# Linear-recurrence block on one core: paired 64x64 tiles for two products, narrower powers, and work moved between engines

## What is computed

```
xx  = shift(x) - x
lo  = tanh((x + xx*maa_x) @ maa_w1)            # 4 groups of 32
xm[g] = x + xx * (lo[g] @ maa_w2[g] + maa[g])  # four mixed inputs: rg, wa, k, v
r, k, v = xm_rg @ Wr, xm_k @ Wk, xm_v @ Wv     # 512x512 each
g = tanh(xm_rg @ gate_w1) @ gate_w2 ;  w, a, ma, mk, kk: low-rank gates and a normalised key
step:  sa = S a ;  S = S * w + sa b^T + v k^T ;  y = S q      # S: 32x32 per head
y = group_norm(y) * ln_w + ln_b + (sum(r*k*faaaa)) * v
out = feed_forward(y * g @ Wo)                 # layer norm, int8 rows, 512x512, scale, bias, residual
```

## Time and profile before

| | |
|---|---|
| median of 3 runs | 3234.14 us (3229.86 to 3235.64) |
| profiled execution | 3244.0 us, span 3242.2 us |
| PE busy / PEld busy | 3029.1 us (93%) / 2675.6 us (83%), 84224 instructions each |
| DVE / ACT / POOL busy | 2626.5 (81%) / 1974.8 (61%) / 1270.6 us (39%) |
| chain that ended last | PE 92%, issue 3%, ACT 2%, DVE 2% |
| DMA queue of SP | 6.8% of the 16 engines; x tile 128 KB, 2.7 us to landing |
| ACT_TABLE_LOAD | 383 at L504 and 64 at L643, 1283 ns each |

### The profile page before, as it was taken

How to read it: one execution, slowest core, us unless ns; L and a number is a source line. 1 busy time by engine, 2 the same in 40 slices (tenths; PEclk the granted TensorE clock), 3 DMA queues, 4 the chain that set the end, 5 groups by cost and what they waited for, 6 DMA issues and landing times.

```text
span 3242.2 us, 182735 instructions
## 1 busy us (share of the span) xinstructions
PE 3029.1 (93%) x84224; PEld 2675.6 (83%) x84224; DVE 2626.5 (81%) x5443; ACT 1974.8 (61%) x3519; POOL 1270.6 (39%) x1161
## 2 busy tenths in 40 slices
PE   6999999999999999999999999999999999999996
PEld 5888888888888888888888888888888888888884
DVE  4788888888888888887888888887888878888875
ACT  3575675665665665755656656656567566566563
POOL 4334334334334344343344343443433434433332
PEclk9999999999999999999999999999999999999998
DMA  3000000000000000000000000000000000000000
GB/s 118 10 23 20 17 23 19 18 20 18 22 20 17 23 20 17 23 20 17 22 20 19 20 17 23 20 17 23 20 17 23 20 17 20 20 20 20 16 17 19
DMA packets 39380, 70.47 MB, mean 22 GB/s; under 512 B 9812, under 2 KB 10836, under 8 KB 38616
## 3 DMA queue, kind: packets, MB, share of 16 engines
q1 hardware_dynamic: 38616, 58.77, 6.8%
HBM read 41.97 MB, written 16.78 MB: 18 GB/s over the span
## 4 chain that ended last, share of the span: by engine, by line
PE 92%; issue 3%; ACT 2%; DVE 2%; POOL 0%; POOLq 0%; ACTq 0%; DVEq 0%
PE bank L1070 30%; PE bank_a L1209 12%; PE bank L1273 8%; PE bank_a L1187 4%; PE bank L1077 4%; PE bank_b L1187 4%; PE bank_b L1244 3%; PE bank_b L1237 3%; PE bank_a L1237 3%; PE bank_a L1244 3%; PE bank_a L1217 2%; PE bank_a L1225 2%; PE bank L1123 2%; PE bank_a L1263 2%; PE bank_b L1263 2%
## 5 line engine op out<-in xcount | busy, mean ns | idle before, releaser
L504 ACT ACT_TABLE_LOAD x383 | 491.4, 1283 | 19.1 <-DVE shift L761 12.2
L1070 PE MATMUL bank<-xm_rg,w_r 128*128 128x128 f32 x2048 | 285.4, 282 | 4.3 <-issue 3.5
L504 ACT ACTIVATE u<-bank_a,parity 128x256 f32<-128x256 f32 x128 | 53.7, 471 | 386.7 <-PE bank_a L1253 386.7
L1209 PE MATMUL bank_a<-pw,w_ffn_int 32*32 32x64 f32 x16384 | 264.6, 216 | 22.0 <-issue 17.2
L1273 PE MATMUL bank<-w_o,yc 128*128 128x512 f32 x512 | 268.9, 626 | 11.0 <-DVE yc L744 9.3
L1209 PEld LDWEIGHTS bank_a<-pw,w_ffn_int 32*32 32x32 f32 x16384 | 239.6, 106 | 41.7 <-issue 21.3
L1070 PEld LDWEIGHTS bank<-xm_rg,w_r 128*128 128x128 f32 x2048 | 248.9, 191 | 26.8 <-issue 15.9
L504 ACT ACTIVATE u<-bank_b,parity 128x256 f32<-128x256 f32 x128 | 53.8, 471 | 342.3 <-PE bank_b L1253 342.3
L1070 PEld LDWEIGHTS bank<-xm_k,w_k 128*128 128x128 f32 x2048 | 241.2, 194 | 12.5 <-issue 3.8
L1070 PE MATMUL bank<-xm_v,w_v 128*128 128x128 f32 x2048 | 250.2, 275 | 0.0
L1070 PE MATMUL bank<-xm_k,w_k 128*128 128x128 f32 x2048 | 241.7, 277 | 3.5 <-issue 3.5
(11 more groups left out here) (204 smaller groups left out, 8540.4 us busy)
## 6 DMA issues: line engine op xcount, KB each, us to landing
xin<-in_x SPq DMA_DIRECT2D x128, 128.0 KB, 2.7
xres<-in_x SPq DMA_DIRECT2D x128, 128.0 KB
out<-o_sb SPq DMA_DIRECT2D x128, 128.0 KB, 2.4
w_ffn_int<-in_weight_q SPq DMA_DIRECT2D x1, 2048.0 KB, 10.8
w_k<-in_Wk SPq DMA_DIRECT2D x1, 1024.0 KB
w_r<-in_Wr SPq DMA_DIRECT2D x1, 1024.0 KB
w_v<-in_Wv SPq DMA_DIRECT2D x1, 1024.0 KB
w_o<-in_Wo SPq DMA_DIRECT2D x1, 1024.0 KB, 14.2
```

Of the source, the lines that this page charges most:

```text
L504: return nc.scalar.activation(out_, in_, func, **kw)
L1070: ins = mm(bank[:, o * n:(o + 1) * n], weights[:, k, o * P:(o + 1) * P], x[:, k].rearrange("p b t -> p (b t)"), start=(k == 0), stop=(k == ...
L1209: ins = mm(bank_a[q, 64 * n:64 * n + 64], pt[q, g, :], source[q, g, 0:2].rearrange("p j t -> p (j t)"), start=True, stop=True)
```

## The change

On TensorE:

1. `scores` replaces `scores_b` and `scores_k`. For each group the two key products follow the two removal products, and they write the other half of the partitions of bank_b, so that the four products of a group stand in four different 64x64 tiles. `scores` now waits for both a_b2 and a_k2 at its start.
2. `first_state_second_values` interleaves, in the same way, the state products of chunk 0 (bank_b) with the value products of chunk 1 (bank_a). `first_values` and `second_state` stay alone.
3. The powers stream 32 columns (k = 0) and 48 columns (k = 1, 2) instead of 64; `pw` is [P, G, 3, HALF].
4. The order of the step is rearranged.

So that the operands lie where the off-diagonal tiles want them, Wv is loaded with its 64-column halves swapped (8 DMAs instead of 1), and two new pairs of DMAs per step on SP (`turn_keys`, `turn_values`) move kt and vT_raw to the other half of the partitions.

On the other engines: ScalarE expands each square into `spread` (two passes with a mask as scale) beside the copy pw, so that VectorE transposes from there; it adds maa for three of the four mix factors (12 passes of 128 columns), and VectorE keeps one multiply for each; it computes x2n with a bias that VectorE forms (`norm2_shift`). GpSimd forms the first sums (two adds), and tx. The orders of VectorE, ScalarE and GpSimd are rearranged too; in ScalarE's, `log_variance` and its function set come ahead of the `keys` copy, and `exp_tables` (a table load) stands between `solution(m, 0)` and `output_gate`.

```diff
-            def scores_b(m):
+            def scores(m):
                 pe.wait_ge(v_q, count(m, 1, 1))
                 pe.wait_ge(a_b2, count(m, 1, 1))
+                pe.wait_ge(a_k2, count(m, 1, 1))
                 pe.wait_ge(a_y, count(m, NC, 0))
-                scores(bank_a, bt2).then_inc(p_sb, 1)
...
+                for g in range(G):
+                    for h in range(QH // 2):
+                        q = two_heads(h)
+                        removal = mm(bank_a[q, 64 * g:64 * g + 64], both(bt2[q, g]), both(aq[q, g, 0:2]),
+                                     start=True, stop=True)
+                    for h in range(QH // 2):
+                        q = two_heads(h)
+                        key = mm(bank_b[other(q), 64 * g:64 * g + 64], both(kt2[q, g]), both(aq[q, g, 0:2]),
+                                 start=True, stop=True)
+                removal.then_inc(p_sb, 1)
+                key.then_inc(p_sk, 1)
...
+                    if k == 0:
+                        ins = mm(bank_a[q, 64 * n:64 * n + CHUNK], pt[q, g, :], first[q, g, 1, :], start=True, stop=True)
+                    else:
+                        ins = mm(bank_a[q, 64 * n:64 * n + 3 * HALF], pt[q, g, :],
+                                 pw[q, g].rearrange("p a t -> p (a t)"), start=True, stop=True)
...
+            def first_state_second_values(m):
+                pe.wait_ge(sold, count(m, NC, 1))
+                pe.wait_ge(v_t, count(m, 1, 1))
+                pe.wait_ge(p_values, count(m, 1, 1))
+                for j in range(GS):
+                    for h in range(QH // 2):
+                        ins = state_product(0, j, two_heads(h))
+                    for h in range(QH // 2):
+                        values_product(1, j, two_heads(h))
+                ins.then_inc(p_rhs, 1)
...
             def power(m, k):
                 act.wait_ge(p_pw, count(m, POWERS, k + 1))
-                run(pw[:, :, 0, :], pairs(bank_a)[:, :, 0, :], ACT.Copy).then_inc(a_pw, 1)
+                square = pairs(bank_a)[:, :, 0, 0:HALF]
+                act.wait_ge(v_ptT, count(m, POWERS + 1, k + 1))
+                run(spread[:, :, 0, :], square, ACT.Identity, scale=mask_half[:, 0:1])
+                run(spread[:, :, 1, :], square, ACT.Identity, scale=mask_half[:, HALF:HALF + 1]).then_inc(a_spread, 1)
+                run(pw[:, :, 0, :], square, ACT.Copy).then_inc(a_pw, 1)
...
+            def mix_factors(i, n):
+                act.wait_ge(p_xm, count(i, 1, 1))
+                act.wait_ge(mix_loaded, MIX_LOADED)
+                g = (1, 2, 3, 0)[n]
+                for k in range(KB):
+                    ins = run(xm[n][:, k], fb[MIX_BANK[n]][:, k * TOK:(k + 1) * TOK].rearrange("p (b t) -> p b t", b=B),
+                              ACT.Identity, bias=maa[:, g, k:k + 1])
+                ins.then_inc(a_xm, 1)
...
+            def turn_keys(i):
+                sp.wait_ge(v_k, count(i, 1, 1))
+                sp.wait_ge(v_klT, count(i, 1, 0))
+                for h in range(2):
+                    sp.dma_start(kt_turned[other(two_heads(h))], kt[two_heads(h)]).then_inc(k_turned, 16)
```

371 lines of the change are left out of this document (215 added, 156 removed).

## The result

The changed kernel takes **3374.48 us**, median of 4 runs (3353.67 to 3378.91), against 3232.0 us (3225.11 to 3235.64) for the kernel before on the same chip: ratio 1.0436, interval 1.0393 to 1.0479. Slower by 142 us, where 155 us faster was forecast. The profiled execution took 3353.67 us, the fastest of the four, with a span of 3352.0 us and a mean granted clock of 0.955; the others had 0.948 to 0.950. Before, the profiled execution had 0.992.

A forecast was written before the change was run, and what follows sets the result against it. The prediction took the order of TensorE's instructions as the bound: 4.78 us less work minus 2.3 us more waits gives 2.5 us per step, 155 us over 62 steps, so 3080 us, range 2985 to 3238.

The forecast's parts named there:

- TensorE's own work: Powers 1.40, scores 1.92, state and values 1.46 us less: TensorE's work falls by 4.78 us per step.
- The disputed step: Scores, state and values: two tiles on the same rows overlap, giving -1.92 and -1.46 us per step; 0 if not.
- The powers: Fewer streamed columns: first power -0.70 us, the other two -0.35 each, together -1.40 us per step.
- mixed_inputs' wait: TensorE's mixed_inputs waits for ScalarE's copy of the output gate from its bank: 0.7 us per step, new.
- The clock: TensorE's clock, fully granted before; below 1.00 in the steady part was listed as a sign of being wrong, without a cost.
- Holes without releaser: TensorE's idle places with no visible releaser, 34.9 us over the span at the powers alone, taken as unchanged.
- The other waits: TensorE's waits per step: gates 0.6, power 0 0.7, powers 1 and 2 0.1 and 0.4, solve_step 1 0.64, quantised 0.35 us.
- kraw: The gates on TensorE wait for ScalarE's copy of kraw: 0.6 us per step.
- rhs: solve_step 1 on TensorE waits for the right-hand sides of chunk 1: 0.64 us per step, as before.
- The DMA moves and GpSimd: SP's four more DMAs a step and GpSimd's three products of at most 1.06 us: nothing on TensorE waits for them.
- The rival with most of the chance of a slower kernel: No overlap of tiles on the same rows: 3.38 us a step come back, 3251 us; chance 0.20, 0.14 of it slower.
- Late engines: Other engines set the step: new waits twice as long, +2.0 us a step, 3200 us; chance 0.16, slower 0.03.

The follow-up runs named there:

- e1: The changed kernel without the exp_tables preload in ScalarE's step: 3187.79 us, ratio 0.9851 to the kernel before.
- b1: The kernel before with only the exp_tables preload moved between solution(m, 0) and output_gate: 3441.92 us, ratio 1.0688.
- e7: The changed kernel with two redundant 512-column products on TensorE ahead of mixed_inputs' wait for hid_g: 3300.38 us, ratio 1.0207 to the kernel before.
- e10: e1 with all three powers streaming 64 columns again: 3200.18 us, ratio 0.9884 to the kernel before.
- e3: e1 with scores and state with values issued bank by bank, only two tiles used at a time: 3250.03 us, ratio 1.004 to the kernel before.
- e4: e1 without the four DMAs a step of turn_keys and turn_values, operands read where they lie: 3192.57 us, ratio 0.987 to the kernel before.
- e8: e1 with one redundant 512-column product between scores and gates: 3195.03 us, ratio 0.9869 to the kernel before.
- e11: e1 with two redundant 512-column products between scores and gates: 3208.49 us, ratio 0.9907 to the kernel before.
- b2: The kernel before with only the four tiles for scores and state with values, no operand moves: 3334.59 us, ratio 1.0335.
- b4: The kernel before with 2048 extra matmul instructions of 16 columns at TensorE's start, to time instruction arrival: 3279.91 us, one execution.

## Why the prediction was wrong, step by step

**TensorE's own work: right.** The disputed step, two tiles on the same rows, came out at the end that was taken: scores 3.88 to 2.10 us, state and values 5.96 to 4.54 in e1, where the clock is nearly undisturbed (-1.8 and -1.4 against -1.92 and -1.46). The weight loads of the 64x64 tiles take 136 ns in the scores, 135 before, so the second tile on a row group has its load beside the first one's products. The Trainium skill, TensorE: Matmul & The Clock Gate, section Part 3, which says that a load overlaps products in flight only where the row group differs, doesn't describe this; TensorEngine Tiling (Array Packing), section Tiling Modes, does. The powers gave 2.05 - 1.31 = 0.74 and 3.96 - 3.38 = 0.58, together 1.32 against 1.40. In the sum of e1 (47.06 - 43.71 = 3.35) 1.4 us of the 4.78 are missing: the clock's 1.62 - 0.24, halved, is 0.7 of it.

**mixed_inputs' wait: the step that failed.** The text put 0.7 us for the copy of the gate, and had the row of the tanh with its table load in hand, but let it stand "behind it in ScalarE's queue", as if nobody on TensorE waited for it. The code waits for a_hg as well. One more load (1.28) and the tanh (0.28) make 0.7 into 2.2. The cost was thus read for the engine that executes (8 loads a step, as forecast) and not for who waits at its end.

**The clock: the assumption that failed.** It was named as what would be wrong ("a clock below 1.00 in the steady part because TensorE has holes now"), but stood in the sum at nothing and in the rivals nowhere. By half of its time it costs about 1.9 us a step in the kernel after. b1 and e7 show it from both sides.

**Holes without releaser: "unchanged" failed.** They doubled, 1.15 to 2.38 us a step. They were taken as given, but had a cause that the change touches: blocks of 256 instructions that come no faster than about one in 3.6 us. Of the change's own parts the narrower powers account for about half of the growth (0.62 in e10). What made the other 0.6, whether the new order around gates and power 0 or something else, these runs leave open: neither two tiles for scores, state and values (e3, 2.31), nor the DMA moves (e4), nor time ahead of the gates (e8, e11) changed it. Four tiles can make such holes, though: alone, in the old order, they raised them to 1.88 (b2).

**The other waits** were forecast well: kraw 0.6 and measured 0.70, rhs 0.64 and 0.64, mask 0.7 and 0.38; powers 1 and 2 and quantised, 0.85 together, hardly waited. The DMA moves and GpSimd were free as said; busy GpSimd is 1259.16/2800 x 51.1 = 23.0 us a step, against 19.9 + 3 x 1.06 = 23.1 worked out.

**The sum of the misses.** Of 4.2 us a step, idle time is 6.33 - 2.33 = 4.0 where 2.3 was forecast: 1.7, which is 1.5 more for hid_g, 1.2 for the holes, less about 1.0 for waits that were smaller. Work fell by 2.43 where 4.78 was forecast: 2.35, of it up to 1.9 clock; the rest, some 0.5 (0.7 in e1), are small amounts at many stages, such as 3.58 to 4.04 us at the values and 3.90 to 4.20 at the queries, whose cause I didn't follow. The rival with most of the chance of a slower kernel was the overlap, which held. Late engines had 0.03 for it, and by their own bound: idle time did grow by 4.0, nearly the 4.3 given there, but that alone would leave a gain of 0.8 us a step. What came was a wait, its clock and the supply of instructions, and the latter two stood in no rival.

The fastest version measured is e1, which beats both kernels: the change without its preload, 0.9851 (0.9818 to 0.9884) of the time before.

## What to carry to other kernels

Before a function set's preload is moved, follow every table load it brings to the first wait of the bottleneck engine behind it, and go through all semaphores that this stage waits for, not only the newest. A hole in TensorE costs more than its length: put into the sum the low clock behind it (here about half as much again). And where TensorE runs many short products, count its instructions too: below about 28 ns for a matmul instruction with its load (3.6 us for 128), over a whole block, a saving in columns comes back as holes.

## What the runs showed of the hardware

Four 64x64 tiles in float32, two of them on each row half, keep 60 ns per instruction and tile, 128 instructions of 64 columns in 1.9 us. Instructions reach TensorE in blocks of 256, one packet of 16384 bytes each, one in 3.5 to 4.0 us in a quiet stretch and in 6.2 us or more beside large loads, with 223 matmul instructions in hand at first (b4); TensorE goes on about 1.4 us after the packet has landed, and an edge reached too early leaves a hole of up to 2.8 us in the steady part (after, e1) with no releaser in the profile. And a single hole of 2.2 us in a step of some 50 was enough to bring the clock down from 2.4 to 1.2 GHz in many of the steps: in b1, where nothing else was changed, 42 of the 43 drops in its 61 full steps stand at that hole, and in the kernel after 31 of 61, with the others behind holes without releaser.
